# A four-layer attention stack on one core: statistics step by step, expert rows issued by GpSimd, five context elements before the expert tiles, and the next attention begun during the gather

## The reference

```
L0: x += mha(ln(x), ln(x));  x += mha(ln(x), ln(ctx))
    h = ln(x); logits = h @ router.T; vals, idx = top_k(logits, 2); gates = softmax(vals)
    x += sum_k gates[k] * (gelu(h @ fc1[idx[k]].T + b1) @ fc2[idx[k]].T + b2)      # 8 experts, 1024 wide
L1: x += mha_causal(ln(x)); x += mlp(ln(x)); x += mha(ln(x), ctx); x += mlp(ln(x))  # gelu
L2: rms norms, 4 kv heads, q and k normed: cross attention, swiglu, self attention, swiglu
L3: rms norms, rope: cross attention, silu MLP
```

## Time and profile before

| | us |
|---|---|
| median of three runs | 2075.71 |
| lowest and highest | 2063.17, 2079.53 |
| the profiled execution's own time | 2073.06 |
| its span, first to last instruction | 2071.1 |
| PE busy | 1774.1 (86%) |
| DVE, ACT, POOL busy | 1323.0, 866.2, 617.3 |
| mixture, from the last update before it to the last of its own | 367 to 642 |

### The profile page before, as it was taken

One profiled execution on the slowest core, in us unless ns is written; L12 is line 12 of the kernel. 1 busy time (PEld: TensorE's weight loads), 2 busy tenths in 40 slices (PEclk: granted clock), 3 DMA queues, 4 the chain that ended last, 5 costly groups with the idle time before them and its releaser, 6 DMA issues.

```text
span 2071.1 us, 34242 instructions
## 1 busy us (share of the span) xinstructions
PE 1774.1 (86%) x10630; PEld 1235.5 (60%) x10630; DVE 1323.0 (64%) x3354; ACT 866.2 (42%) x2513; POOL 617.3 (30%) x711
## 2 busy tenths in 40 slices
PE   5959998689986868989779999896897979998988
PEld 4746665578874657555565555384444845555567
DVE  5856667311106886888665776796777966656555
ACT  3735554232324642565224444343332445445421
POOL 2325555200012233676320000130000325555434
PEclk9979999789998988999698999998999999999989
DMA  4100000478863000002100020011000100000100
GB/s 166 36 16 16 15 7 15 146 244 282 303 198 106 1 0 30 30 32 70 66 8 16 16 68 0 0 51 61 1 0 4 69 1 12 22 11 23 59 1 18
DMA packets 38632, 115.07 MB, mean 56 GB/s; under 512 B 2960, under 2 KB 26032, under 8 KB 31360
## 3 DMA queue, kind: packets, MB, share of 16 engines
q1 hardware_dynamic: 32520, 101.63, 14.5%
q10 hardware_dynamic: 4472, 8.45, 1.2%
q0 software_dynamic: 1536, 3.67, 0.6%
HBM read 99.34 MB, written 14.40 MB: 55 GB/s over the span
## 4 chain that ended last, share of the span: by engine, by line
PE 42%; issue 21%; POOL 15%; DVE 13%; DMA 4%; ACT 4%; POOLq 0%; SPq 0%; DVEq 0%; ACTq 0%
POOL arena L1978 12%; PE ps L982 7%; PE ps L1022 4%; PE ps L796 3%; PE ps L848 3%; PE ps L902 3%; PE ps L1141 3%; PE ps L791 3%; DMA arena<-rows_hbm 2%; PE ps L1125 2%; PE ps L922 2%; PE ps L866 2%; PE ps L838 1%; PE ps L908 1%; ACT arena L1240 1%
## 5 line engine op out<-in xcount | busy, mean ns | idle before, releaser
L1978 POOL TENSOR_TENSOR arena<-arena,rinv 112x375 f32<-112x375 f32 (+1 forms) x448 | 371.2, 830 | 498.7 <-DVE rinv L1640 486.2
L866 PEld LDWEIGHTS ps<-cst,arena 112*125 112x125 f32 (+1 forms) x1408 | 190.4, 186 | 181.1 <-POOL arena L1978 90.5
L866 PE MATMUL ps<-cst,arena 112*125 112x112 f32 (+1 forms) x1408 | 249.0, 296 | 48.6 <-POOL arena L1978 45.7
L1262 ACT ACTIVATE arena<-ps,negmax 112x375 f32<-112x375 f32 (+1 forms) x384 | 190.6, 502 | 173.0 <-DVE negmax L1635 172.6
L1649 DVE COPY arena<-ps 125x336 f32<-125x336 f32 x384 | 190.5, 497 | 50.4 <-PE ps L866 48.9
L1635 DVE TENSOR_REDUCE negmax<-ps 112x1 f32<-112x375 f32 (+1 forms) x288 | 157.9, 548 | 74.9 <-PE ps L838 65.9
L2026 POOL TENSOR_TENSOR w_split_sb<-wml,w_split_sb 128x512 fp32r<-128x512 f32 (+1 forms) x40 | 45.7, 1142 | 529.2 <-ACT w_split_sb L1328 527.3
L982 PE MATMUL ps<-h_split_sb,w_split_sb 128*128 128x448 f32 x768 | 180.0, 383 | 16.9 <-DVE h_split_sb L1524 6.2
L1262 ACT ACTIVATE arena<-arena,negmax 112x112 f32<-112x112 f32 (+1 forms) x256 | 125.4, 491 | 133.0 <-DVE negmax L1624 90.4
L982 PEld LDWEIGHTS ps<-h_split_sb,w_split_sb 128*128 128x128 f32 x768 | 151.3, 199 | 35.0 <-DVE h_split_sb L1524 12.9
L791 PE MATMUL ps<-wat,arena 128*125 128x256 f32 (+1 forms) x608 | 152.5, 388 | 8.2 <-ACT arena L1206 7.3
(11 more groups left out here) (217 smaller groups left out, 3150.3 us busy)
## 6 DMA issues: line engine op xcount, KB each, us to landing
wml<-in_wm_L_moe SPq DMA_DIRECT2D x21, 1028.0 KB, 5.6
wml<-in_wm_L_moe SPq DMA_DIRECT2D x21, 1024.0 KB, 7.1
craw<-in_ctx SPq DMA_DIRECT2D x34, 375.0 KB
wml<-in_wm_L_m SPq DMA_DIRECT2D x3, 3072.0 KB, 13.7
wat<-in_wa_L_ca SPq DMA_DIRECT2D x2, 2560.0 KB, 10.2
wml<-in_wm_L_m SPq DMA_DIRECT2D x2, 2048.0 KB, 10.1
keys_hbm<-arena ACTq DMA_DIRECT2D x8, 375.0 KB
values_hbm<-vz ACTq DMA_DIRECT2D x8, 375.0 KB
```

What stands on the lines that cost most here:

```text
L866: last = nc.tensor.transpose(ps[0:blk.kp, T_BANK + s % blk.t_banks, o:o + S], buf[:, i * blk.nk + q * blk.kp:i * blk.nk + (q + 1) * blk.kp ...
L1262: last = go(probs[0:S, s % blk.nprobs, i * nk:(i + 1) * nk], src[:, i * nk:(i + 1) * nk], ACT.Exp, scale=-1.0 if blk.mask == "input" else ...
L1978: pool.tensor_tensor(p3, p3, r3, ALU.mult).then_inc(scaled, 1)
```

## The change

- **Statistics.** The chain for the next block is cut into 13 steps (`statistic_step`), and covers elements 0 to 5. In body(7) step j runs at unit `s` with `j * units // 13 == s`, one link at a time. Elements 6 and 7 go together in body(8). Before the mixture, the first six elements are also normalised in body(8), once the last copy is done.
- **Expert rows.** POOL issues the loads of the tiles' rows, behind the scatter, into six buffers instead of two (`ROWS_AHEAD`).
- **Context.** Five elements come before the tiles (`FIRST_AHEAD`), none between them, three after. Their loads and stores move from ACT's queue to SP's, between the first expert weights. The weights of block 3 are asked for at tile 19.
- **Next attention.** The statistics and norm of element 0 come right after its own gather, those of 1 to 7 at the start of the attention. PE's first pieces no longer wait for all eight elements. So that the attention can write, the gather's destinations move to parts that it doesn't use.
- **Banks.** `OUT_BANKS` leaves out bank 5.

```diff
+ROWS_AHEAD = 6
+FIRST_AHEAD = 5
...
-        OUT_BANKS = (0, 1, 2, 3, 5, 4, 6, 0)
+        OUT_BANKS = (0, 1, 2, 3, 4, 6, 0, 1)
...
+                def load_ahead(m):
+                    sp.wait_ge(ahead_done, NAHEAD * m + AHEAD_NAMES.index("CT1") + 1)
+                    sp.dma_start(craw[:, m % 2], ctx[m + 2].rearrange("(k p) d -> p k d", p=KP)).then_inc(ahead_loaded[m % 2], 16)
+
+                def store_ahead(m):
+                    sp.wait_ge(ahead_done, NAHEAD * (m + 1))
+                    sp.dma_start(keys_hbm[m], kT_ahead[:, m % 2]).then_inc(ahead_stored[m % 2], 16)
+                    sp.dma_start(values_hbm[m], v_ahead[:, m % 2]).then_inc(ahead_stored[m % 2], 16)
+
                 sp.wait_ge(rows_zeroed, 32)
+                for m in range(2):
+                    load_ahead(m)
+                    store_ahead(m)
                 sp.wait_ge(experts_known, 1)
-                for t in range(2):
-                    load_w1(t)
-                sp.wait_ge(scattered, 16 * TOP * B)
-                for t in range(2):
-                    load_rows(t)
-                for t in range(2):
-                    load_w2(t)
+                load_w1(0)
+                load_ahead(2)
+                store_ahead(2)
+                load_w2(0)
+                load_ahead(3)
+                load_w1(1)
+                store_ahead(3)
+                load_w2(1)
+                load_ahead(4)
+                store_ahead(4)
                 for t in range(NT + 1):
+                    if t == NT - 2:
+                        load_attn(n + 1)
                     if t + 2 < NT:
                         sp.wait_ge(tile_act, 2 * (t + 1))
                         load_w1(t + 2)
-                        load_rows(t + 2)
...
-                    elif bank < T_BANK:
+                    elif bank < T_BANK and n and isinstance(BLOCKS[n - 1], Attn):
                         wait(pe, out_done, st["out"])
                     piece(0, name, None)
-                wait(pe, out_done, st["out"])
+                if n and not (isinstance(BLOCKS[n - 1], Mlp) and BLOCKS[n - 1].experts > 1):
+                    wait(pe, out_done, st["out"])
...
-                    if b == B - 1:
+                    if OUT_BANKS.index(OUT_BANKS[b]) < b:
                         pe.wait_ge(out_done, st["out"] + OUT_BANKS.index(OUT_BANKS[b]) + 1)
...
                 last.then_inc(gt_full, 1)
+                context_ahead(4)
...
-                    if t == NT - 3:
-                        pe.wait_ge(tile_act, 2 * (NT - 2))
-                        pe.wait_ge(tile_kept, NT)
-                        context_ahead(4)
-                        pe.wait_ge(ahead_done, 5 * NAHEAD)
-                for m in range(5, B):
+                pe.wait_ge(tile_act, 2 * NT)
+                for m in range(FIRST_AHEAD, B):
                     context_ahead(m)
                 pe.wait_ge(ahead_done, B * NAHEAD)
+                pe.wait_ge(tile_out_kept, NT)
...
-                behind = n > 0 and isinstance(BLOCKS[n - 1], Mlp) and BLOCKS[n - 1].experts == 1
+                behind = n > 0 and isinstance(BLOCKS[n - 1], Mlp)
...
+                        if s == lag and b == B and isinstance(BLOCKS[n + 1], Mlp) and BLOCKS[n + 1].experts > 1:
+                            dve.wait_ge(scored, START[n + 1]["unit"])
+                            normalise_tokens(n + 1, 0, SOON)
...
                                 take_updated(b + -1)
 
+                            if b == B:
                                 tail = Links(links[0].base + links[0].k)
-                                statistics(tail, n + 1, 0 if b == B - 1 else B - 1, b)
+                                statistics(tail, n + 1, 2 * SOON, b)
                                 after[0] += tail.k
+                        if b == B - 1 and n + 1 < len(BLOCKS):
+                            known = links[0].k
+                            for j in range(2 + ROOT_STEPS):
+                                if j * units // (2 + ROOT_STEPS) == s:
+                                    statistic_step(links[0], n + 1, 0, 2 * SOON, j)
+                            after[0] += links[0].k - known
...
                     take(b, X[:, b])
-                    if b == B - 2:
-                        statistics(link, n + 1, 0, B - 1)
-                statistics(link, n + 1, B - 1, B)
+                    if b == 0:
+                        statistics(link, n + 1, 0, 1)
+                        normalise(xn[:, :], X[:, 0], BLOCKS[n + 1].kind, rstd8[:, 0:1], mv8[0:S, 0, 0:1]).then_inc(xn_ready, 1)
...
+                pool.wait_ge(scattered, 16 * TOP * B)
+                for t in range(NT):
+                    if t >= ROWS_AHEAD:
+                        pool.wait_ge(tile_turned, t - ROWS_AHEAD + 1)
+                    pool.dma_start(tile_rows[:, t % ROWS_AHEAD], rows_hbm[t * P:(t + 1) * P]).then_inc(rows_in[t % ROWS_AHEAD], 16)
                 for i in range(2):
                     pool.wait_ge(tile_stored[i], 16 * ((NT + 1 - i) // 2))
```

More of the change, by code:

```diff
@@ L374, in build @@
         tile_out = in_arena(2 * D).rearrange("p (t d) -> p t d", t=2)
-        results = in_arena(TOP * B * D, S).rearrange("p (b k d) -> p b k d", b=B, k=TOP)
         b2_sb = in_arena(D, E)
+        cn_at = list(sizes).index("cn")
+        cn_at = sum(list(sizes.values())[:cn_at])
+        cT_at = cn_at + sizes["cn"] + sizes["hT"]
+        assert mlp_at[0] <= cn_at and sizes["cn"] >= TOP * D and a0 - cT_at >= (B - 2) * TOP * D and 2 * T >= TOP * D
+        spare = mask_sb[:, :, :].rearrange("p t k -> p (t k)")
+        results = [arena[0:S, cT_at + b * TOP * D:cT_at + (b + 1) * TOP * D] for b in range(B - 2)] + [arena[0:S, cn_at:cn_at + TOP * D], spare[:, 0:TOP * D]]
+        results = [r.rearrange("p (k d) -> p k d", k=TOP) for r in results]
         gates = sb("gates", [S, E, B])
@@ L442, in build @@
         w2_in = [sem("w2_in0"), sem("w2_in1")]
-        rows_in = [sem("rows_in0"), sem("rows_in1")]
+        rows_in = [sem(f"rows_in{i}") for i in range(ROWS_AHEAD)]
         tile_turned, tile_kept = sem("tile_turned"), sem("tile_kept")
@@ L725, in _ @@
                     load_mlp(n)
-                elif n >= 3 and n != AHEAD_AT:
+                elif n >= 4 and n != AHEAD_AT:
                     load_attn(n)
@@ L1149, in output_bias @@
                     mm(ps[0:S, bank, D:2 * D], gT[:, b * S:(b + 1) * S], b2_sb, start=True, stop=True).then_inc(out_full, 1)
-                pe.wait_ge(ahead_done, 4 * NAHEAD)
+                pe.wait_ge(ahead_done, FIRST_AHEAD * NAHEAD)
                 turn_tile(0)
@@ L1423, in mixture @@
                             last.then_inc(tile_act, 1)
-                    if t == NT - 2:
-                        context_ahead(4)
-                for m in range(5, B):
+                for m in range(FIRST_AHEAD, B):
                     context_ahead(m)
@@ L1490, in take, with statistic_step @@
                            stat8[0:S, bass.ds(b.i * 2 + b.o, 1)].rearrange("p o j -> p (o j)"), x).then_inc(taken, 1)
+            def statistic_step(link, n, b0, b1, j):
+                blk = BLOCKS[n]
+                if j == 0:
+                    dve.wait_ge(taken, B * n + b1)
+                    for b in range(b0, b1):
+                        last = v.bn_aggr(mv8[0:S, b], stat8[0:S, b])
+                    link(last)
+                elif j == 1 and blk.kind == "rms":
+                    link(v.tensor_tensor(newton[0:S, b0:b1], mv8[0:S, b0:b1, 0], mv8[0:S, b0:b1, 0], ALU.mult))
+                    link(v.scalar_tensor_tensor(var[0:S, b0:b1], mv8[0:S, b0:b1, 1], blk.eps, newton[0:S, b0:b1], ALU.add, ALU.add))
+                elif j == 1:
+                    link(v.tensor_scalar(var[0:S, b0:b1], mv8[0:S, b0:b1, 1], blk.eps, None, ALU.add))
+                else:
+                    root_step(link, rstd8, S, b1, b0, j - 2)
             def statistics(link, n, b0, b1):
@@ L1496, in statistics @@
                     return
-                blk = BLOCKS[n]
-                dve.wait_ge(taken, B * n + b1)
-                for b in range(b0, b1):
-                    last = v.bn_aggr(mv8[0:S, b], stat8[0:S, b])
-                link(last)
-                if blk.kind == "rms":
-                    link(v.tensor_tensor(newton[0:S, b0:b1], mv8[0:S, b0:b1, 0], mv8[0:S, b0:b1, 0], ALU.mult))
-                    link(v.scalar_tensor_tensor(var[0:S, b0:b1], mv8[0:S, b0:b1, 1], blk.eps, newton[0:S, b0:b1], ALU.add, ALU.add))
-                else:
-                    link(v.tensor_scalar(var[0:S, b0:b1], mv8[0:S, b0:b1, 1], blk.eps, None, ALU.add))
-                rsqrt(link, rstd8, S, b1, b0)
+                for j in range(2 + ROOT_STEPS):
+                    statistic_step(link, n, b0, b1, j)
             def normalise_tokens(n, p0, p1):
@@ L1826, in mixture @@
                 link = Links(chain[0])
-                for b in range(B):
-                    last = normalise(xnA[:, b], X[:, b], blk.kind, rstd8[:, b:b + 1], mv8[0:S, b, 0:1])
```

(3 more changed lines are left out.)

46 lines of the change are left out of this document (26 added, 20 removed).

## The result

| | kernel before | kernel after |
|---|---|---|
| median (range), 11 runs each | 2072.94 (2063.17 to 2079.53) | 2052.03 (2047.26 to 2058.77) |
| profiled execution: time, span | 2073.06, 2071.1 | 2057.58, 2055.8 |
| mean granted clock | 0.931 | 0.932 |

The ratio is 0.9911 [0.9895, 0.9927]: 21 us are won, where 55 were forecast, and 2052.0 lies above the range's end of 2045. A later set of runs gave 2050.2 and 0.9893 [0.9846, 0.9941].

What follows compares the result with a forecast made beforehand. PE, busy 86% of the span, was taken to bound the kernel; only its waits and half clock could go. Gains of 2 + 7 + 13 + 9 + 22 + 2 = 55 us gave a forecast of 2020.7 us, range 2003 to 2045.

Steps and rivals of the forecast that it cites:

- Statistics: Ends of seven attentions: spreading the chains removes 33.5 us of chain and half clock, links cost 11.5; gain 22 us.
- the half clock, 12.5: Slow clock behind the seven chains: 5 us in L1_ca, 2.5 in L0_ca, 5 in the other five together.
- Five context elements first: Ahead of the tiles: element 4 is covered by the wait for tile 0's rows, element 3's stall goes; gain 7 us.
- Rival 4: Context loads still wait behind weights, element 4 gains 0, block 3's keys hold the attention: 2031.7 us; chance 0.10.
- Banks: Second pieces of L2_ca and L2_sa no longer wait for bank 5; gain 2 us, bounds 0 and 5.
- Rows: Expert tiles: POOL's queue and six buffers remove row waits and slow results; gain 13 us, bounds 4 and 16.6.
- the 3.6 that I gave back for weights: Tiles: half of the 7.6 us of later row waits was expected to come back as waits for `w1`.
- rival 1: Tiles: weights take the place of rows, gain 7.6 instead of 13, 2026 us; sign: over 6 us of `wml` waits; chance 0.17.
- The next attention: After the gather: first mask 7 us behind the last addition instead of 14; gain 9 us, bounds 5 and 11.
- Entry: Entry of the mixture: six elements normalised earlier in a DVE gap; gain 2 us, bounds 0 and 2.7.
- Rival 2: Attentions: the statistics only move, DVE being full where links land; gain 3 instead of 22, 2039.7 us; chance 0.12.
- Rival 3: Attentions: link delays run round the loop of four engines, 1.0 us a link; slower than before, 2103 us; chance 0.03.

Runs made afterwards that it cites:

- run 1: Kernel after, with the next block's statistics again in one chain of seven elements and one of the eighth: 2056.1 us, 0.9929.
- FILL = 95: Kernel after, with 95 one-element memsets among the tiles that only move DVE's later code: 2044.4 us, 0.9861.
- its repeat: Kernel after, unchanged, measured and profiled once more: 2050.2 us.
- run 2: Kernel before, with the spread statistics alone: 2070.8 us, 0.9993.
- run 3: DVE's code moved by memsets: 95 on the kernel after, 2044.4 us; 33 on the kernel after with single-chain statistics, 2066.4 us.
- run 5: Kernel after, element 4's context load ahead of the first expert weight, later context loads and stores behind tiles 3 and 7: 2038.6 us, 0.9851.
- run 6: Kernel after, with six row buffers but SP asking for rows: 2041.6 us; with two buffers and GpSimd asking: 2046.8 us.
- run 8: Kernel after, with the early begin of L1_sa undone (statistics, norm, Q and keys late, as before): 2057.4 us, 0.9927.
- FILL = 40: Kernel after, with 40 memsets among the tiles, so L3_ca's loop begins at instruction 2611: 2049.4 us in one run.
- run 7: Four context elements ahead of the tiles instead of five: on the kernel after 2045.5 us; on the combined kernel 2040.3, against 2029.6 with five.

## Why the prediction was wrong

The direction was right and every place named did change. Three steps of the sum failed.

- **Statistics, forecast 22.** Gained: 11 to 14 at equal place of the code, and of that 7 to 10 were taken back by the loop of L3_ca, which the sum had no term for. Net about 4. Inside the 11 to 14, runs 1 and `FILL = 95` can be compared step by step. The last steps of the seven attentions are 20.1 us shorter, which is the chains' 21. The steps in which the links now stand are 4.4 longer, where I had 11.5 as paid; some 2 to 5 us more are lost elsewhere. What fails is the half clock, 12.5: none of it shows. In L1_ca the clock did come back, but the time hardly did: in its last step the stretch at half clock shrinks from 31.2 us in before to 12.6 in after, and the step from 33.7 to 28.5, of which the chain alone is 3.0 (windows of after; us, busy per engine, PEclk):

```profile
971.00:979.00 8.00, 6.34 (x55) 3.76 (x53) 7.79 (x23) 3.81 (x13) 4.06 (x6) 1.00 0.00 0
979.00:987.00 8.00, 5.64 (x50) 3.50 (x50) 7.83 (x22) 3.66 (x12) 4.66 (x6) 0.99 0.01 3
```

  DVE is busy for 15.6 of 16 us and PE idle for 4: at full clock DVE is the bound of these units. The earlier trace rows had said so with 0.86, which I used for the links and not for the clock. Elsewhere no time shows either: from element 5's row to 7's L0_ca takes 47.7 us in run 1 and 47.9 with `FILL = 95`. L2_sa's two slow elements, 5.8 us, are in after, in its repeat and in run 2, in neither of before and run 1, and only one of them in `FILL = 95`. Even so the spread is not their cause: run 3's kernel with one chain and 33 memsets has both, and runs 5, 6, 8 and `FILL = 40` have the spread and neither. They go with a late entry. In the eleven profiles whose first row of L2_sa comes 52.9 us or more after the row ahead of it at least one element is slow (21.0 to 22.4 us instead of 19.5), in the seven with 52.6 or less none is. What sets that entry is open.
- **Five context elements first, forecast 7.** The cover that I worked out exists (10.6 us in run 7), but I followed the element's loads through SP's queue and not its stores. "SP now stands on `ahead_done` with expert weights behind it" looked at `w1(1)` alone. The context stood behind `w1(0)`, the keys' store blocked SP for 10.17 us, and `w1(2)` paid. As written the term is -6.5 (-11.8 by the ratios). Rival 4 had this, with 0 as its price and a chance of 0.10.
- **Banks, forecast 2.** It gave nothing or cost 1 to 3. I counted the waits of the first pieces and not what hangs on the last transposes, SP's order for keys and values.
- **Rows, forecast 13.** No wait for rows is left. What remains of the 21 us when the other terms are taken off (2.4, -6.5, 5.4, 4, -2) is 18, just above my upper bound of 16.6; no run undoes the rows alone. The timelines give nearly the same. Before, the tiles take 187.2 us from the first turn at 423.20, 7.2 of them element 4, so 180.0. After, they take 177.4 from 423.11 (I had said about 155), of which 14.6 are the wait for `w1(2)` and the slow hidden layer behind it, so 162.8: 17.2 less. What failed in this term is the 3.6 that I gave back for weights. My sign for rival 1, more than 6 us of waits for `wml`, was a bad test: 14.0 us came, but 11.9 of them at one tile, which SP's order set (run 5). Rival 1 itself falls: it had a shortage in every tile, and behind tile 2 only one weight is waited for, by 1.1 us. The rule weighed in the prediction, from the Trainium skill ("DMA: Bandwidth & Descriptors", section "Issuing engines are not separate DMA queues"), agrees with run 6: with six buffers on SP's queue no later tile waits for rows.
- **The next attention, forecast 9.** 6.8 us at the place, 5.4 in the time: right within its bounds.
- **Entry, forecast 2.** 2.4 in the profile.

Rival 2 names the net of the statistics (3 for 4) but not its cause. Rival 3 did not occur.

## What to carry to other kernels

Give a transfer's store the same care as its load: whatever a store can block on its queue belongs in the sum. When an edit changes the number of instructions on an engine with long loops, look in the profile of after for idle time with no releaser and for more fetches in that engine's instruction queue, and shift the code before judging the edit. An experiment that undoes an edit moves the code too.

## What the runs showed of the hardware that was not expected

**A loop can pay for where it lies.** DVE's loop of 320 instructions in L3_ca either shows no gap in its three turns or one at each of its two back branches, by a start 33 instructions apart; each is 2.5 to 3.5 us long with packets of the instruction queue inside it, and the kernel loses 7 to 10 us in all. A packet of this queue has 8 KB (0.48 MB in 59). DVE's shorter loops (81 to 202 instructions) show no gap at any start tried. The Trainium skill ("Runtime: NRT & Kernel Launch", section "Instruction fetch mechanics") says that a taken branch to a place outside the window of fetched code stalls for the fetch; the traces agree in kind. No run here shows how large that window is.

**An issue on SP can take 10 us with the DMA engines not full.** While the keys' store stood in its issue from 423.08 to 433.25, the DMA engines were busy for 0.79 of 424 to 428, but then only for 0.42 of the next stretch and 0.62 of the one that ends behind it (windows of after, last columns DMA share and GB/s):

```profile
428.00:432.00 4.00, 3.00 (x27) 2.77 (x26) 0.73 (x2) 2.40 (x10) 0.54 (x1) 1.00 0.42 154
432.00:436.00 4.00, 4.00 (x27) 3.72 (x26) 0.73 (x2) 2.00 (x8) 0.54 (x1) 1.00 0.62 213
```

What it stood on in these is open; no run separates the number of transfers ahead of it from their sizes.

**The same gap of PE does not always cost the same clock.** Between the rows of elements 1 and 2 of L2_sa PE waits 1.48 us in both kernels. After it the 8 matmuls of `Q` take 3.69 us before and 5.34 after, and so again in the repeat. What PE did earlier differs only in time, and not in work. One such difference is on record, the entry to the block (52.0 us before, 53.1 after); why the clock falls in the one and not in the other is open.
